# A two-layer graph network on one core: layer 1's outputs in two PSUM banks, its receivers' one-hot rows on ScalarE, filler matmuls behind its sums

## The reference, cut to what matters

```python
h = jnp.maximum(_layernorm(x, axis=-1), 0.0)
logits = (h @ var_u)[src] + (h @ -var_u)[dst] + var_c     # 8 per edge
q = softmax(logits)
x_sep = h[dst] * edge_weight[:, None]
for m in range(8):
    agg = segment_sum(q[:, m:m+1] * x_sep, src, num_segments=3125)
    y = y + agg @ var_w[m]
x = x + y + var_b
```

## Time and profile before

| what | value |
|---|---|
| median of three runs | 2352.28 us (2349.9 to 2352.87) |
| profiled execution | 2348.29 us, of which the span 2346.5 us is in the trace |
| busy over the span: PE, DVE, ACT, POOL | 1665.7, 1420.8, 556.3, 1622.2 us |
| layer 0's loop, roughly | 100 to 1080 us |
| layer 1's loop, roughly | 1180 to 2330 us |

### The profile page before, as it was taken

How to read it: one execution, slowest core, us unless ns; L and a number is a source line. 1 busy time by engine, 2 the same in 40 slices (tenths; PEclk the granted TensorE clock), 3 DMA queues, 4 the chain that set the end, 5 groups by cost and what they waited for, 6 DMA issues and landing times.

```text
span 2346.5 us, 53388 instructions
## 1 busy us (share of the span) xinstructions
PE 1665.7 (71%) x9941; PEld 1160.7 (49%) x9941; DVE 1420.8 (61%) x6157; ACT 556.3 (24%) x1978; POOL 1622.2 (69%) x1700
## 2 busy tenths in 40 slices
PE   3888889998988999889745555555555655555555
PEld 2555555555555555555434444444444544444444
DVE  6344343444444444443268888888888888888885
ACT  2333333333333333333111111111111111111110
POOL 3777777777777777774467667676767676767673
PEclk8899898989899999999555555555555555555555
DMA  3544444444444444442243333333333333333332
GB/s 87 115 102 98 91 104 92 101 97 101 93 101 98 97 98 96 98 95 61 63 102 93 91 92 91 91 91 91 94 90 93 91 93 91 94 89 93 91 92 57
DMA packets 353332, 216.98 MB, mean 92 GB/s; under 512 B 284830, under 2 KB 325881, under 8 KB 353056
## 3 DMA queue, kind: packets, MB, share of 16 engines
q0 software_dynamic: 66800, 113.26, 21.1%
q1 hardware_dynamic: 284822, 102.20, 18.1%
q10 hardware_dynamic: 1684, 1.24, 0.2%
HBM read 209.80 MB, written 6.69 MB: 92 GB/s over the span
## 4 chain that ended last, share of the span: by engine, by line
DVE 29%; issue 26%; POOL 19%; PE 12%; DVEq 7%; DMA 6%; ACT 0%; POOLq 0%; SPq 0%; ACTq 0%
POOL X L583 18%; DVE EQW L1145 4%; DMA X<-table_src,slot_s 4%; DVE EQW L1151 3%; DVEq L1210 3%; DVE OT L995 2%; PE bank L1368 2%; DVE EX L1191 2%; DVE r L1183 2%; PE bank L1351 2%; DVE r L1187 2%; DVE r L1178 2%; DVE OE L1196 2%; PE bank L1377 2%; DVE sT L1212 2%
## 5 line engine op out<-in xcount | busy, mean ns | idle before, releaser
L591 POOL DMA_INDIRECT G<-table_node_and_list,slot_s x825 | 795.6, 964 | 374.5 <-issue 211.2
L583 POOL DMA_INDIRECT X<-table_src,slot_s x825 | 787.0, 954 | 288.9 <-issue 272.0
L1479 PE MATMUL bank<-Q,G 125*64 125x128 f32 x1650 | 416.6, 425 | 180.9 <-DVE Q L1204 180.9
L1479 PEld LDWEIGHTS bank<-Q,G 125*64 125x64 f32 x1650 | 314.8, 222 | 193.9 <-issue 125.0
L1009 DVE TENSOR_TENSOR sT<-sT,bank 65x16 f32 x275 | 46.2, 168 | 550.3 <-PE bank L1387 511.5
L1351 PE MATMUL bank<-filler 128*128 128x384 bf16 x1100 | 374.2, 340 | 2.4 <-issue 2.4
L1490 PE MATMUL bank<-R,w_z 65*64 65x64 f32 x1104 | 133.9, 316 | 279.1 <-DVE sT L1212 279.1
L995 DVE TENSOR_SCALAR OT<-KBT,base_p 48x375 bf16<-48x375 int32 x550 | 232.8, 424 | 68.7 <-issue 37.9
L1490 PEld LDWEIGHTS bank<-R,w_z 65*64 65x64 f32 x1104 | 122.9, 224 | 283.2 <-issue 283.2
L1368 PE MATMUL bank<-XT,w_ex 128*64 128x375 f32 x550 | 249.6, 537 | 4.7 <-issue 4.7
L1377 PEld LDWEIGHTS bank<-w,H 65*125 65x125 f32 x1650 | 230.2, 198 | 0.0
(11 more groups left out here) (165 smaller groups left out, 2006.9 us busy)
## 6 DMA issues: line engine op xcount, KB each, us to landing
KBT<-in_dst SPq DMA_DIRECT2D x550, 70.3 KB, 2.1
X<-in_edge_attr SPq DMA_DIRECT2D x275, 93.8 KB
HK<-keys SPq DMA_DIRECT2D x275, 93.8 KB
X<-table_src,slot_s POOLq DMA_INDIRECT x825
G<-table_node_and_list,slot_s POOLq DMA_INDIRECT x825
BW<-table_dst_parts SPq DMA_DIRECT2D x275, 6.0 KB
UW<-table_logit_src_parts SPq DMA_DIRECT2D x275, 0.8 KB, 1.6
table_node_and_list<-sm SPq DMA_DIRECT2D x1, 1562.5 KB
```

The source lines that it names most:

```text
L583: pool.indirect_dma_start(X[:, j, q, D:2 * D], None, tA, bass.IndirectOffsetOnAxis(ap=slot_s[:, j, q:q + 1], axis=0)).then_inc(gat_a[0][j] ...
L591: pool.indirect_dma_start(G[:, j, q, :], None, tH, bass.IndirectOffsetOnAxis(ap=slot_s[:, j, q:q + 1], axis=0)).then_inc(g_gather[j], 16)
L1479: last = pe.matmul(bank[2 + j % 2][0:D, 0:WM], G[0:P, j, q, 0:D], Q[:, j % 2, q].rearrange("p m n -> p (m n)"), start=(q == 0), stop=(q == ...
```

## The change

Three edits in layer 1. The counters, loops and steps of layer 0 stay.

1. **Outputs in two banks.** `outputs_w` and `add_outputs` use bank 6 or 7 by the turn's parity `u`; `outputs_w` waits for the adds of the turn before the last. For the parity to be known, PE and DVE loop over pairs of turns (`over_pairs`). The `value_load` of `add_outputs` becomes a step of its own, `output_place`, behind `window_weights`; the add itself goes to the end of the pass.
2. **One-hot rows from ScalarE.** `OT` is no longer made by DVE but by two ACT instructions two groups ahead: `OD = |base_p - KBT|` (`Abs`), then `OT = max(0, 1 - OD)` (`Relu`), with a new counter `u_D` between them. SP reloads `KBT` after `u_D`.
3. **Fillers.** PE issues four `fill(bank[0])` at the end of each group's pass, behind `aggregate_w`.

```diff
+        def over_pairs(eng, body, depth):
+            for s in range(2 * RB):
+                body(s // RB, s % RB, s // RB % 2)
+            with eng.Fori(1, TURNS // 2) as i:
+                for u in range(2):
+                    for j in range(RB):
+                        body(2 * i + u, j, u)
+            for s in range(TURNS * RB, NG + depth):
+                body(s // RB, s % RB, s // RB % 2)
...
             def rows1w(t, j):
                 g = RB * t + j
-                done(sp, u_OT, t, j, RB)
+                done(sp, u_D, t, j, RB)
...
+            def window1_t(t, j):
+                act.wait_ge(kbt_load[1][j], (t + 1) * 16)
+                done(act, u_OT, t, j, 1)
+                act.activation(OD[:], KBT[:, j, :], ACT.Abs, bias=base_p[:, bass.ds(RB * t + j, 1)], scale=-1.0
+                               ).then_inc(u_D, 1)
+
+            def window1_one(t, j):
+                done(act, u_D, t, j)
+                done(act, u_U, t, j, RB)
+                act.activation(OT[:, j, :], OD[:], ACT.Relu, bias=one_col[:, 0:1], scale=-1.0).then_inc(u_OT, 1)
...
             def body1w(t, j):
                 back(exps_w, t, j, 1)
                 back(neighbours_w, t, j, 2)
+                back(window1_t, t, j, -2)
+                back(window1_one, t, j, -2)
...
-            def add_outputs(t, j):
+            place = {}
+
+            def output_place(t, j):
+                place["at"] = dve.value_load(first_of[0:1, bass.ds(RB * t + j, 1)], min_val=0, max_val=N - WG)
+
+            def add_outputs(t, j, u):
                 dve.wait_ge(u_y, t + 1)
                 done(dve, u_acc, t, j, 1)
-                first = dve.value_load(first_of[0:1, bass.ds(RB * t + j, 1)], min_val=0, max_val=N - WG)
-                to = yT[:, bass.ds(first, WG)]
-                dve.tensor_tensor(to, to, bank[6][0:D, j * WG:(j + 1) * WG], ALU.add).then_inc(u_acc, 1)
+                to = yT[:, bass.ds(place["at"], WG)]
+                dve.tensor_tensor(to, to, bank[6 + u][0:D, j * WG:(j + 1) * WG], ALU.add).then_inc(u_acc, 1)
...
-            def body1w(t, j):
-
-                back(lambda t, j: window_t(1, t, j), t, j, 0)
+            def body1w(t, j, u):
+
                 back(window_places, t, j, 2)
-                back(add_outputs, t, j, 2 * RB)
                 back(exp_sums, t, j, 2)
...
                 back(window_weights, t, j, 2)
+                back(output_place, t, j, 2 * RB)
                 back(reverse_edges, t, j, 1)
...
                 back(logits_less_max, t, j, 1)
+                back_pair(add_outputs, t, j, 2 * RB, u)
...
-            def outputs_w(t, j):
+            def outputs_w(t, j, u):
                 if j < RB - 1 and not (isinstance(t, int) and RB * t + j == NG - 1):
                     return
                 done(pe, u_R, t, j)
-                if not isinstance(t, int) or t > 0:
-                    pe.wait_ge(u_acc, RB * t)
+                if not isinstance(t, int) or t > 1:
+                    pe.wait_ge(u_acc, RB * (t - 1))
                 for m in range(M):
-                    last = pe.matmul(bank[6][0:D, 0:RB * WG], w_z[:, m, :], R[:, m].rearrange("c j n -> c (j n)"),
+                    last = pe.matmul(bank[6 + u][0:D, 0:RB * WG], w_z[:, m, :], R[:, m].rearrange("c j n -> c (j n)"),
...
-            def body1w(t, j):
+            def body1w(t, j, u):
                 back(logits_w, t, j, 0)
-                back(outputs_w, t, j, 3)
+                back_pair(outputs_w, t, j, 3, u)
                 back(aggregate_w, t, j, 2)
-
-            over_groups(pe, body1w, DEPTH1)
+                for _ in range(4):
+                    fill(bank[0])
+
+            over_pairs(pe, body1w, DEPTH1)
```

More of the change, by code:

```diff
@@ L169, in build_gnn @@
         KBT = sb("KBT", [WP, RB, GE], I32)
+        OD = sb("OD", [WP, GE])
+        one_col = sb("one_col", [WP, 1])
         OT = sb("OT", [WP, RB, GE], BF16)
@@ L267, in build_gnn @@
                                     "scale", "head", "OH"))
+        u_D = sem("u_D")
         u_Q, u_agg, u_R, u_y, u_acc = (sem(f"u_{n}") for n in ("Q", "agg", "R", "y", "acc"))
@@ L357, in back, with back_pair @@
                 step(tk, jk)
+        def over_pairs(eng, body, depth):
[7 more added lines that the diff above has]
+                body(s // RB, s % RB, s // RB % 2)
+        def back_pair(step, t, j, k, u):
+            jk = (j - k) % RB
+            dt = (j - k - jk) // RB
+            if not isinstance(t, int) or 0 <= RB * (t + dt) + jk < NG:
+                step(t + dt, jk, (u + dt) % 2)
         def done(eng, counter, t, j, k=0):
@@ L823, in body1w @@
                 back(neighbours_w, t, j, 2)
+                back(window1_t, t, j, -2)
+                back(window1_one, t, j, -2)
             for j in range(RB):
                 slots_w(1, 0, j)
+            for j in range(2):
+                window1_t(0, j)
+                window1_one(0, j)
             over_groups(act, body1w, DEPTH1)
@@ L879, in _ @@
             dve.memset(eps_col[:], EPS)
+            dve.memset(one_col[:], 1.0)
             dve.memset(no_key[:], -1.0)
@@ L990, in group0, with window_t @@
                                 ).then_inc(dve_g[0], 1)
-            def window_t(l, t, j):
-                dve.wait_ge(kbt_load[l][j], (t + 1) * 16)
-                done(dve, (f_h1, u_U)[l], t, j, RB)
+            def window_t(t, j):
+                dve.wait_ge(kbt_load[0][j], (t + 1) * 16)
+                done(dve, f_h1, t, j, RB)
                 dve.tensor_scalar(OT[:, j, :], KBT[:, j, :], base_p[:, bass.ds(RB * t + j, 1)], None,
-                                  ALU.is_equal).then_inc((f_OT, u_OT)[l], 1)
+                                  ALU.is_equal).then_inc(f_OT, 1)
             def window_e(t, j):
@@ L1023, in body0w @@
             def body0w(t, j):
-                back(lambda t, j: window_t(0, t, j), t, j, 0)
+                back(window_t, t, j, 0)
                 back(same_next, t, j, 2)
@@ L1238, in body1w @@
                 back(logits_less_max, t, j, 1)
+                back_pair(add_outputs, t, j, 2 * RB, u)
             dve.wait_ge(yT_zero, 1)
-            over_groups(dve, body1w, DEPTH1)
+            over_pairs(dve, body1w, DEPTH1)
             dve.wait_ge(u_found, NG)
```

## The result

The changed kernel takes 2294.24 us (median of four runs, 2291.66 to 2298.13) where the kernel before takes 2351.18 in the same comparison: a ratio of 0.9759, 95% interval 0.9742 to 0.9776. That is 57 us or 2.4% faster; 72 were forecast, and the time lies inside the range. The profiled execution took 2291.66 us.

What follows compares the result with a forecast made beforehand. DVE's order of steps was taken to bound layer 1: 0.44 + 0.17 - 0.35 = 0.26 us saved per group, times 275 is 72 us, so 2352.28 - 72 = 2280.8, forecast 2281 us, range 2248 to 2316.

Steps and rivals of the forecast that it cites:

- What bounds the kernel: Layer 1: DVE's order of steps sets the pace, 4.149 us per group; POOL's limit is 3.77 to 3.82.
- `L` to `r`: DVE's stretch between these steps in layer 1: 0.47 instead of 0.91 us, ended by `EX`, 0.44 saved per group.
- `Q` to `EQW`: DVE's stretch now holding the register load: 0.83 instead of 0.48 us, 0.35 lost; bounds 0 and 0.45, with an additional register row.
- The branch's 0.59: Loop branch on DVE: this part covered by the wait for `EX`; with the 0.20 behind `r`, 0.17 us per group saved.
- the other two stretches: DVE's `r` to `Q`, forecast to change by -0.02 us per group, and `EQW` to the next `L`, by 0.
- The second bank: PE's wait of 248.9 us for the adds goes; PE and POOL do not set the pace, so costed at nothing.
- The fillers: Four on PE per group, 0.32 us each, PE 3.59 of 3.89 us: costed at nothing; bounds 0 and 0.52 each.
- ACT: hidden: Two added ACT instructions, 0.96 us per group, lie in ACT's idle time, with slack 2.8 or 1.1 us before `EX`.
- POOL as the bound: Rival: the load hides under `Q`, POOL paces at 3.77 to 3.82 us per group, 2248 to 2262 us; chance 0.25.
- The gain eaten: Rival: `EX` late behind ACT's new instructions in half the passes, 0.24 us per group lost, 2347 us; chance 0.06.
- PE as the bound: Rival: fillers take 0.52 us each at 1.2 GHz, PE needs 4.39 us per group, 2418 us; chance 0.05.
- One sign of being right: In layer 1, POOL's gathers would wait for ACT's index copies hardly at all, where they had waited 118.8 us.

## Why the prediction was right, and where it was off

**What bounds the kernel.** Right for the order of DVE's steps: the saving in `L` to `r` and the loss in `Q` to `EQW` make up the result, stretch by stretch. Right too, as far as an estimate shows it, that PE's 248.9 us behind `add_outputs` cost the kernel before little: some 10 us by the estimate above, and at most the 37 us that two banks and the loop over pairs gained together. What I missed is that the change's second edit makes this wait dear: with the one-hot rows in ACT's queue, the chain of add, `outputs_w`, `aggregate_w`, index copy and `EX` grows by ACT's 1.21 us, and with one bank it holds the period at 4.13 to 4.14, although DVE is spared the compare (3.99 with the one-hot rows ahead of the copy).

***L* to *r*: right.** 0.47 was forecast, 0.467 came, ended by `EX`. The branch's 0.59 is covered there as taken (0.505 in the passes behind the branch, 0.46 in the others); the 0.04 beyond the forecast is mostly that the mean of before, 1.098, was above what one ordinary pass and a quarter of the branch make (0.91 + 0.15).

***Q* to *EQW*: the mis-sized term.** A loss of 0.35 was taken with 0.45 as the upper bound, 0.42 came. The rows of the load have the durations of the earlier trace rows to the nanosecond in the median (changed kernel, line 1246):

```profile
L1246 DVEq FUSED_REGOPS  x539: 53/190/196, 1210.4 to 2272.6; - x180
L1246 DVEq TENSOR_LOAD <-first_of x275: 300/305/323, 1210.5 to 2272.2; - x138
L1246 DVEq SEQ_ASSERT  x275: 23/23/23, 1211.1 to 2272.8; - x138
```

So the load costs what it did, and what I had too low was the time around it. Half of the passes need 0.86 us, near the 0.83 of the prediction; the other half need 0.97, as the 0.96 in the timeline above. In three of eight the trace has the additional register row there, which I kept as a bound; in one of eight it has no such row, and why that one is long stays open. 0.07 x 275 = 19 us, more than the whole miss of 13 (72 - 58.8); the 0.04 of `L` to `r` gave 11 back, and the other two stretches took some 7.

**The second bank: the step that failed.** "Neither set the pace, so I cost it at nothing" holds for the kernel before and fails for the change. The forecast came out near because it summed DVE's order alone, which only the second bank makes the limit. That the change has both edits made the omission harmless; this part was luck, since the prediction named earlier index copies as the bank's gain and gave them no price. Without it the same edits give 2348 with load and add at the head (2274 with it), and 2630 as the change places them (2294 with it).

**The fillers: right.** No cost and no gain in layer 1, with 0, 4 and 8. In the trace the starts of four lie 0.29 to 0.32 us apart, as the earlier trace rows had it, and the last ends 1.46 us after the first starts (1702.79 to 1704.25, the row below); PE has room.

```profile
1702.79 1.46 PE L1391 MATMUL bank<-filler 128*128 128x384 bf16 x4
```

**ACT: hidden, as forecast, at a higher price.** The two instructions, from the page of the changed kernel:

```profile
L842 ACT ACTIVATE OT<-OD,one_col 48x375 bf16<-48x375 f32 x275 | 167.3, 608 | 29.5 <-ACT OD L836 9.4
L836 ACT ACTIVATE OD<-KBT,base_p 48x375 f32<-48x375 int32 x275 | 166.9, 607 | 18.3 <-DMA KBT<-in_dst 18.2
```

1.21 us instead of 0.96. The Trainium skill, "ScalarE: Activation LUTs", section "What ACT_TABLE_LOAD costs", has a longer start for an instruction whose bias is read from a column: as an estimate by that page 280 + 0.833 x 375 = 592 ns, and 607 and 608 were measured, so the trace agrees; the row that I took it from is of an instruction without such a column (line 750). The rule that the prediction cites from the Trainium skill, max, add and the like on VectorE ("ScalarE: Activation LUTs", section "Rules for kernel authors"), agrees with the trace in engine time, 0.41 us against 1.21. For the kernel's time it is not borne out here: with the compare on VectorE it takes 2330 us, on ScalarE 2294. 1.21 us on an engine with room is cheaper here than 0.41 on the one that paces.

**The rivals.** POOL as the bound was the nearest: the floor of 3.82 is there and was reached with the load at the head (3.816) and without it (3.817), at 2261 to 2274 us, and nearly so with the load at the end (3.838). "The gain eaten" by a late `EX` did not happen with two banks, but it is what happens with one. PE as the bound did not come near. One sign of being right did not come: gathers were to wait for ACT's copies hardly at all, and waited 55.2 us, 0.23 per group; DVE never waited for a gather to land.

## What to carry to other kernels

A wait on an engine that does not pace is harmless only as long as nothing that the pacing engine needs stands close behind it: follow the chain from the wait through each engine's queue round to the pacing engine, and when an edit lengthens a queue on that chain, price the two together (here two edits, 0.5% and 1.6% alone, made 3.4%). The register load held DVE for 0.3 to 0.4 us in every place tried, so put such a load where the next step waits for something else anyway; here another place for it gave 1.1% beyond the change (2269 against 2294).

## What was not expected of the hardware

- The register load (0.7 us of sequencer rows) holds DVE for nearly the same time in every place, in the mean of the waits: 0.35 us behind `Q`, 0.35 in the kernel before (one pass of 0.22 stands in the earlier trace rows), 0.32 at the end of the pass, 79.2 / 215 = 0.37 at the head. What its place changes is what else runs meanwhile: against 0.476 and 0.461 without a load in the stretch, it lengthens `Q` to `EQW` by 0.43 behind `Q`, and `L` to `r`, where `EX` is on its way, by 0.35 at the end and 0.30 at the head.
- TensorE's granted clock in layer 1 was 0.50 (1.2 GHz) with no filler, 0.65 with four and 0.97 (nearly always 2.4 GHz) with eight per group, and layer 1 took the same time within 3 us: matmuls at nearly twice the clock brought nothing here, where PE has room.
